# Audio tower kernel: attention and output weights loaded to the place of their low parts, the second chunk's norm split, one reciprocal moved

## What is computed

```python
h = xf @ W_proj + b_proj                     # token layer
y = layernorm(h) * ln_g + ln_b
w = softmax((y @ W_wgen + b_wgen).reshape(B, T, 8, 5))
conv = einsum('kbthr,bthk->bthr', taps(y), w)
h = h + relu(conv @ W_ff + b_ff)

x = layernorm(h)                             # attention, 8 heads of 64
q, k, v = split(x @ w_qkv.T + b_qkv)
attn = softmax(causal(einsum('bhfc,bhtc->bhft', k, q)), axis=-2)
h = h + (einsum('bhft,bhfc->bhtc', attn, v) @ w_o.T + b_o)

h = h + block_diagonal_ffn(layernorm(h))     # 16 blocks, GELU
```

## Time and profile before

| | |
|---|---|
| median of 3 runs | 1031.34 us (1030.89 to 1031.8) |
| the profiled execution's own time | 1035.96 us |
| its span | 1034.2 us |
| TensorE busy | 967.4 us, 94% of the span |
| VectorE, ScalarE, GpSimd busy | 509.2, 424.4, 394.3 us |
| mean granted TensorE clock | 0.977 of full speed |

### The profile page before, as it was taken

The page is one execution under the profiler, slowest core; times in us unless marked ns, Lnnn a source line. Parts: engine busy times, 40 slices in busy tenths (PEclk is TensorE's granted clock), DMA queues, the critical chain, the costliest instruction groups (busy, mean ns, idle before and its releaser), DMA issues.

```text
span 1034.2 us, 15644 instructions
## 1 busy us (share of the span) xinstructions
PE 967.4 (94%) x6108; PEld 714.5 (69%) x6108; DVE 509.2 (49%) x848; ACT 424.4 (41%) x753; POOL 394.3 (38%) x317
## 2 busy tenths in 40 slices
PE   7999999987899999999879999999999999889996
PEld 5777777776777788778657877877887777323331
DVE  6153535659447502254756256256064567755551
ACT  6144444555433533434243243243132332356553
POOL 1225252227601122723361451451023377748532
PEclk9999999999899999999989999999999999899998
DMA  8542725395343154327100201200214975533421
GB/s 290 209 165 4 205 7 181 4 285 203 117 145 107 62 126 164 109 95 265 41 11 22 92 11 35 79 11 22 92 52 149 289 260 209 184 111 133 149 77 61
DMA packets 75062, 124.96 MB, mean 121 GB/s; under 512 B 29159, under 2 KB 38375, under 8 KB 70894
## 3 DMA queue, kind: packets, MB, share of 16 engines
q1 hardware_dynamic: 68830, 107.03, 33.7%
q0 software_dynamic: 5120, 16.78, 4.6%
q10 hardware_dynamic: 1040, 0.16, 0.1%
HBM read 81.46 MB, written 42.50 MB: 120 GB/s over the span
## 4 chain that ended last, share of the span: by engine, by line
PE 53%; issue 10%; POOL 7%; DVE 5%; DMA 3%; ACT 2%; another core or an unknown queue 1%; POOLq 0%; SPq 0%; DVEq 0%; ACTq 0%
PE bank L299 14%; PE bank L301 13%; PE bank L300 13%; PE bank L1795 3%; PE bank L1804 3%; POOL vacc L335 2%; PE bank L1551 1%; POOL out L758 1%; POOL acc L363 1%; DVE sq L377 1%; DMA stage<-w_qkv_t 1%; POOL acc L308 1%; DVE acc L1219 1%; PE bank L1523 1%; DMA db_late<-h_s 1%
## 5 line engine op out<-in xcount | busy, mean ns | idle before, releaser
L335 POOL TENSOR_TENSOR vacc<-vacc,sq 128x512 f32<-128x512 f32 x72 | 97.2, 1350 | 45.8 <-ACT sq L381 36.4
L299 PE MATMUL bank<-xa_h,wp_h 128*128 128x512 f32 x256 | 103.4, 404 | 7.2 <-DVE xa_l L1094 7.2
L299 PE MATMUL bank<-cv_h,wf_h 128*128 128x512 f32 x256 | 106.3, 415 | 1.2 <-POOL wf_l L293 1.2
L301 PE MATMUL bank<-cv_h,wf_l 128*128 128x512 f32 x256 | 101.4, 396 | 0.0
L300 PE MATMUL bank<-cv_l,wf_h 128*128 128x512 f32 x256 | 101.4, 396 | 0.0
L300 PE MATMUL bank<-xa_l,wp_h 128*128 128x512 f32 x256 | 101.1, 395 | 0.0
L301 PE MATMUL bank<-xa_h,wp_l 128*128 128x512 f32 x256 | 101.1, 395 | 0.0
L700 POOL TENSOR_TENSOR fo<-fo,res 128x512 f32<-128x512 f32 x32 | 43.5, 1373 | 123.4 <-ACT fo L837 89.8
L1077 ACT ACTIVATE gt<-bank 128x512 f32<-128x512 f32 x128 | 66.2, 600 | 39.0 <-PE bank L1795 36.8
L1795 PE MATMUL bank<-dd,up_f 64*128 64x512 f32 x256 | 67.9, 651 | 5.6 <-ACT gt L1077 5.4
L381 ACT ACTIVATE sq<-sq 128x512 f32<-128x512 f32 x56 | 35.1, 632 | 79.3 <-DVE sq L377 79.3
(11 more groups left out here) (179 smaller groups left out, 2167.5 us busy)
## 6 DMA issues: line engine op xcount, KB each, us to landing
xs<-x_t SPq DMA_DIRECT2D x32, 256.0 KB, 6.2
h_s<-ho SPq DMA_DIRECT2D x8, 1024.0 KB, 5.9
res<-h_s SPq DMA_DIRECT2D x32, 256.0 KB, 3.6
h_s<-fo SPq DMA_DIRECT2D x32, 256.0 KB, 2.4
dc<-h_s SPq DMA_DIRECT2D x4, 2048.0 KB, 9.3
h<-h_s SPq DMA_DIRECT2D x8, 1024.0 KB, 10.5
h_s<-h SPq DMA_DIRECT2D x8, 1024.0 KB, 4.8
stage<-w_qkv_t SPq DMA_DIRECT2D x24, 256.0 KB, 3.6
```

The source lines that it names most:

```text
L299: pe.matmul(o, wh, xh, start=start, stop=False)
L301: return pe.matmul(o, wl, xh, start=False, stop=stop)
L335: g.tensor_tensor(vacc[:, :], t[:, 0, :] if k == 1 else vacc[:, :], t[:, k % 2, :], ALU.add).then_inc(ln_pool, 1)
```

## The change

Units from 32 on no longer go through `stage`. Each is loaded to the place where its low part will be written (`wv_r`, `wq_r`, `wk_r`, `wo_r` are float32 views of the low parts' places), so nine can be under way (RAW = 9). The places hold w_ff or the convolution's result until the last group of stage B has read them; TensorE counts that in a new semaphore `ff_used`, block by block, and the loads wait for it. Wv and wq have their high and low places exchanged. ScalarE writes the high parts of the first four wv units inside the last group, and those of all wq and wk units ahead of taking v out. `c_values(0)` waits for the first 28 results of stage B instead of all 32; the rest of that wait moves to `c_qk(0, 0)`. The load of chunk 1 comes after all 16 wq and wk units, and no longer after eight. The mean of chunk 1 is taken inside `c_qk(0, 0)`, and four of its eight blocks are centred and squared before q and k of pair 0 are taken out. In every chunk but the last the reciprocal of the next chunk's norm comes after k of pair 2 is taken out.

```diff
-        wv_h = place("wv_h", [P, KB, PART], F32R, R2)
-        wv_l = place("wv_l", [P, KB, PART], F32R, R2 + 16 * KIB)
-        wq_h = place("wq_h", [P, KB, PART], F32R, R2 + 32 * KIB)
-        wq_l = place("wq_l", [P, KB, PART], F32R, R2 + 48 * KIB)
+        wk_r = place("wk_r", [P, KB, PART], F32, R1 + 48 * KIB)
+        wv_l = place("wv_l", [P, KB, PART], F32R, R2)
+        wv_r = place("wv_r", [P, KB, PART], F32, R2)
+        wv_h = place("wv_h", [P, KB, PART], F32R, R2 + 16 * KIB)
...
+        def raw_load(e, u):
+
+            src, _, _, _, raw, dead = units[u]
+            if dead is None:
+                e.wait_ge(v_mm, 4 * CH)
+            elif dead == KB:
+                e.wait_ge(ff_mm, 8 * CH)
+            else:
+                e.wait_ge(ff_used, dead)
+            if u - RAW >= U_V:
+                who = 0 if units[u - RAW][3] == "v" else 1
+                e.wait_ge((w_lo_v, w_lo_g)[who], lo_before[who][u - RAW + 1])
+            e.dma_start(raw, src).then_inc(w_ld[(u - U_V) % RAW], 16)
...
-                if c == CH - 1:
-                    for u in range(U_V, U_V + 4):
-                        unit_load(sp, u)
                 for m in range(KB):
+                    if c == CH - 1:
+                        for u in {4: range(U_V, U_QK), 6: range(U_QK, U_QK + 2), 7: range(U_QK + 2, U_QK + 4)}.get(m, ()):
+                            raw_load(sp, u)
                     ff_store(c, m)
...
-            for u in range(U_V + 4, U_QK + 8):
-                unit_load(sp, u)
+            for u in range(U_QK + 4, U_O):
+                raw_load(sp, u)
             c_load(1)
-            for u in range(U_QK + 8, U_O):
-                unit_load(sp, u)
...
+                if not ahead:
+                    for k in range(4):
+                        act.wait_ge(ff_used, 4 + k // 2 + 1)
+                        unit_hi(act, U_V + k)
...
             c_values(0, range(TILES))
-            for u in range(U_V + 16, U_O):
-                unit_hi(act, u)
+            c_squares(1, range(4))
             c_qk(0, 0)
...
+            c_center(1, range(4))
             c_qk(0, 0)
...
                 if ahead:
-                    c_center(c + 1)
+                    c_center(c + 1, range(KB) if later else range(4, KB))
                 c_qk(c, 1)
                 c_softmax_in(c, 1)
                 c_softmax_out(c, 1)
+                if not ahead:
+                    o_low(0, range(PAIRS))
+                c_qk(c, 2)
                 if ahead:
                     since(v, ln_std, c + 1 + CH, 1, 1)
                     v.reciprocal(rstd[:, :], rstd[:, :]).then_inc(ln_rstd, 1)
-                else:
-                    o_low(0, range(PAIRS))
-                c_qk(c, 2)
...
-            c_qk(0, 0)
+            c_qk(0, 0, lambda: ln_mean_pe(pe, 1 + CH))
```

More of the change, by code:

```diff
@@ L140, in audio_tower @@
         wo_l = place("wo_l", [P, PAIRS, D], F32R, R2 + 16 * KIB)
+        wo_r = place("wo_r", [P, PAIRS, D], F32, R2 + 16 * KIB)
         vs_h = place("vs_h", [P, PAIRS, N], F32R, R1 + 16 * KIB)
@@ L161, in audio_tower @@
         masks_ok = sem("masks_ok")
-        stage_ld = [sem(f"stage_ld{i}") for i in range(4)]
+        w_ld = [sem(f"w_ld{i}") for i in range(RAW)]
+        ff_used = sem("ff_used")
         w_hi = sem("w_hi")
@@ L245, in weight_units @@
                     cols = slice(half * N, half * N + N)
-                    units.append((w_o_t[k * P:(k + 1) * P, cols], wo_h[:, k, cols], wo_l[:, k, cols], "g"))
+                    units.append((w_o_t[k * P:(k + 1) * P, cols], wo_h[:, k, cols], wo_l[:, k, cols], "g",
+                                  wo_r[:, k, cols], None))
             return units
@@ L273, in unit_load @@
             src = units[u][0]
-            e.dma_start(stage[:, u % 4, :], src).then_inc(stage_ld[u % 4], 16)
+            e.dma_start(stage[:, u % 4, :], src).then_inc(w_ld[u % 4], 16)
         def slot_count(u):
@@ L280, in unit_views @@
         def unit_views(u):
-            return stage[:, u % 4, :], units[u][1], units[u][2]
+            raw = units[u][4] if u >= U_V else stage[:, u % 4, :]
+            return raw, units[u][1], units[u][2]
         def unit_hi(act, u):
-            act.wait_ge(stage_ld[u % 4], slot_count(u))
+            unit_landed(act, u)
             st, h, _ = unit_views(u)
@@ L896, in _, with c_squares @@
                 unit_hi(act, u)
-            def c_squares(n):
-                for k in range(KB):
+            def c_squares(n, ks=range(KB)):
+                for k in ks:
                     ln_square_act(act, n + CH, k, dc[:, k, :])
@@ L989, in c_vals @@
                                    bias=vec[:, B_V + m:B_V + m + 1]).then_inc(vo_ev, 1)
-            for u in range(U_V, U_V + 16):
+            for u in range(U_V + 4, U_O):
                 unit_hi(act, u)
@@ L1014, in c_step @@
                 c_softmax_exp(c, 0)
+                if ahead and not later:
+                    c_squares(c + 1, range(4, KB))
                 if later:
@@ L1021, in c_step @@
                 c_pt(c, 0)
-                if ahead and not later:
-                    c_squares(c + 1)
                 c_softmax_exp(c, 1)
@@ L1245, in _, with c_center @@
                 b_step(c)
-            def c_center(n):
-                for k in range(KB):
+            def c_center(n, ks=range(KB)):
+                for k in ks:
                     ln_center_dve(v, n + CH, k, dc[:, k, :], dc[:, k, :])
@@ L1567, in ff_group @@
                         mm.then_inc(ff_mm, 1)
+                if g == 2 and c == CH - 1 and k < KB - 1:
+                    mm.then_inc(ff_used, 1)
             def b_step(c, ahead):
@@ L1620, in c_values @@
             def c_values(c, ts, beside=None):
-                if isinstance(c, int) and c == 0:
-                    pe.wait_ge(ff_ev, 8 * CH)
+                if c == 0:
+                    pe.wait_ge(ff_ev, 8 * (CH - 1) + TILES)
                 elif 2 in ts:
@@ L1645, in c_qk @@
                 first = isinstance(c, int) and c == 0
+                if m == 0 and first:
+                    pe.wait_ge(ff_ev, 8 * CH)
                 if m == 1 or (m == 0 and first):
@@ L1663, in c_qk @@
                         mm.then_inc(xc_used, 1)
-                    if beside and k == 3:
+                    if beside and k == (5 if m == 0 else 3):
                         beside()
@@ L1716, in c_step @@
                     c_values(c, (2, 3))
-                if ahead:
+                if ahead and later:
                     ln_mean_pe(pe, c + 1 + CH)
@@ L1841 @@
 LAST_PREP = {0: (4, 5), 1: (6, 7)}
+RAW = 9
 PREP_AFTER, STAT_FROM, GATHER_AFTER = 3, 5, 4
```

23 lines of the change are left out of this document (17 added, 6 removed).

## The result

The changed kernel takes **1044.95 us**, median of four runs (1040.25 to 1046.14); the kernel before took 1031.12 (1030.55 to 1031.8, four runs). The medians lie 13.8 us apart. The ratio of the runs is 1.0125, with a 95% interval of 1.0105 to 1.0145, which is 12.9 us: slower, and clear of the noise. The forecast was 1041.0 us (1029 to 1047), slower by 9.7, with a chance of 0.73 for slower. The profiled execution took 1046.14 us and is the slowest of the four.

A forecast was written before the change was run, and what follows sets the result against it. TensorE, busy 94% of the span, was taken to bound the kernel. Gains of 10.4 us against 20.1 lost to the moved reciprocal gave +9.7 on a median of 1031.34: 1041.0 us, range 1029 to 1047.

The forecast's parts named there:

- Start of stage C: From stage B's last matmul to the first of `c_values(0)`: the wait goes, 2.3 us gained.
- First q and k group: `c_qk(0, 0)`: no longer starves on low parts, 15.8 us falls to the 10.9 needed, 4.8 us gained.
- Mean of chunk 1: Inside `c_qk(0, 0)`: chunk 1's load issued about 475, sum done at 494, a wait of 0.3 us, up to 3.
- Rival 4: Chunk 1's load lands late and PE waits about 4.5 us at the mean, plus 1.7 slow clock: 1047 us; chance 0.05.
- first case: All terms as summed, the moved reciprocal costing waits and clock: slower, 1041 us (1037 to 1046); chance 0.62.
- Squares ahead of q: Ahead of the first scores: four squares delay q, PE waits 3.0 us instead of 0.94, 2.1 us lost.
- Clock: Behind the new 3.0 us wait ahead of the first scores: a half-speed stretch costs 1.7 us.
- Variance: Variance of chunk 1: the wait of 5.2 us and 2.2 us of lower clock go, 7.4 us gained.
- Moved reciprocal: Ahead of pair 3's scores, chunks 0 to 2: 4.5 us wait plus 2.2 clock each, 20.1 lost; E ends k's take-out.
- Rival 3: Faster: VectorE and GpSimd hardly disturb each other, a chunk loses under 4.0 us; 1024 us (1022 to 1030); chance 0.18.
- Rival 2: The moved reciprocal costs the wait but not the clock: +1.4 us, 1033, up to 1036; chance 0.15.
- Output weights: Their loads wait for the last `c_values`, about 742, and are first read near 758: no effect.

The follow-up runs named there:

- units_ahead: Changed kernel with the reciprocal back in its old place and more q and k units issued ahead of two stage B stores; 1024.9 us, ratio 0.9913.
- ahead_q_first: As units_ahead, with q of pair 0 also taken out ahead of the four squares of chunk 1; 1023.2 us, ratio 0.9901.
- recip_back: Changed kernel with the reciprocal put back ahead of k of pair 2, all else as changed; 1023.0 us, ratio 0.9896 to the kernel before.
- no_lock: Changed kernel with low parts of xc for chunks 1 to 3 subtracting a PSUM bank, so VectorE reads one SBUF input; 1032.1 us, ratio 1.0002.
- fill_pe: Changed kernel with 24 unused matmuls in the wait ahead of pair 3's scores of chunks 0 to 2; 1037.8 us, ratio 1.0046.
- recip_alone: Kernel before with only the reciprocal moved behind k of pair 2; 1053.1 us, ratio 1.0193.
- norm_alone: Kernel before with only the norm of chunk 1 split (earlier mean, four blocks centred and squared early), old weight loads and reciprocal; 1027.4 us, ratio 0.9954.
- q_first: Changed kernel, reciprocal back, chunk 1's load behind the first eight q and k units, first q taken out ahead of four squares; 1021.7 us, ratio 0.9906.

## Why the prediction was right, point by point

The direction, the main term and its three places were right, and the range held the time. The sum was 4.1 us short of the medians and 3.2 short of what the two traces add up to (12.9). The 3.2 come from two terms: the start of stage C gained 8.9 instead of 10.4, and the moved reciprocal cost 21.8 instead of 20.1.

- **Start of stage C**: forecast 2.3 gained. Before, PE went from the last matmul of stage B to `c_values(0)` in 2.61 us, now in 0.23: 2.4. Right.
- **First q and k group**: forecast 4.8. The 36 matmuls ahead of the mean ran without a gap: 487.30 + 36 x 0.228 = 495.5, and the mean started at 498.73 after its wait of 3.11. Right.
- **Mean of chunk 1**: forecast a wait of 0.3, measured 3.1. This is the step that failed. It had SP issue the load of chunk 1 about 475, by ScalarE's pace of 0.63 us for a high part; ScalarE was not the pace: it waited for landings, and SP stood at a store from 464.5 to 468.85. The prediction cost what the wv loads delay "at nothing" and looked only at the residual loads; fourteen units stood behind the stores that wait for those. The queue's part is about 1.2 us by units_ahead and ahead_q_first; for the rest the traces show full DMA engines and low parts at the slow pace, and no run separates the two. Rival 4 of the prediction had named this wait (4.5 us) and gave it 0.05: half of it came true beside the first case, so the prediction was right with this step wrong, because the wait is small beside the main term.
- **Squares ahead of q**: forecast 3.0 of wait instead of 0.94. It was 1.52 (2.45 in recip_back): PE, at the lower clock behind the mean, reached the end of the group later, so part of that wait was already spent. In recip_back the clock behind the mean was full.
- **Clock**: forecast 1.7, behind the wait ahead of the first scores. It was lost behind the mean instead. The mean and the twelve matmuls behind it took 5.3 us (498.73 to 504.07, the end of the group by its last matmul at 503.84) where 0.45 + 12 x 0.228 = 3.2 were needed: 2.1. That this came near the forecast is partly luck: recip_back, with waits of 3.48 and 2.45 in the same places, had full clock behind both. The prediction sorted such waits by length, nothing after 2.22 and a slow stretch after 2.5 or more; over all traces that does not hold under 4 us (last section). The sum of these: 2.4 + 4.8 - 3.1 - 0.6 - 2.1 + 7.5 = 8.9, which is what the two traces show; forecast 10.4.
- **Variance**: 7.4 forecast, 7.5 measured.
- **Moved reciprocal**: forecast 4.5 of wait and 2.2 of clock in each of three chunks, 20.1. Measured 4.9 and 2.4, 21.8. The chain was right step by step (GpSimd from E + 3.3, four low parts beside the last scalings at 1.7, four alone in 2.4, scores at E + 19.1, the late end of the range given). With the strict lock of 1.85 a pair the prediction had 5.6 of waiting a chunk; the pairs took 1.7 and the waiting was 4.9. Rival 3, a loss under 4.0 a chunk, fell with the traces: 7.3. no_lock shows what its premise would have given: two engines that leave each other alone lose 2.0 a chunk in waiting, and the time is that of the kernel before (1.0002), not 1024. Waits of 3.2 that still cost the clock are the likely reason, but only one execution was traced, and it had one such stretch (1.5 us) in three chunks. Rival 2, a wait without the clock, is about what fill_pe measures: 1038, not the rival's 1033, since the start of stage C gained less and the waits were longer.
- **Output weights**: nothing, as forecast. The last scores of chunk 3 stand 254.4 us ahead of the end in the profiled execution of before and 249.9 in that of the changed kernel; but recip_alone and norm_alone, which load them in the old way, have 248.1 and 249.7, and the other ten traces, with the new loads, 247.8 to 250.1. So the 4.5 us are that one execution's own, about the 4.6 by which it lies above its median. They are why the spans of the two traces differ by 10.2 us only: 12.9, and 1.8 from ahead of stage C, less 4.5.

The measured difference (13.8) and the one summed from the traces (12.9) differ by less than the spread of the four runs. One slip of the prediction changes nothing: its first case, by its own terms, runs from 1038 to 1045 and not from 1037 to 1046.

## What to carry to other kernels

An instruction that runs in an idle gap of its engine costs nothing there. Moved out of the gap into the chain, it costs what is left of its length after the slack (here 2.0 us of 3.3), plus what its successors lose when they now run beside an engine that slows them (2.9), plus the clock behind a wait that has grown (2.4). So ask of each move which gap it leaves and what it makes simultaneous; here 3.3 us of work cost 7.3. The version to keep is the change without the move of the reciprocal, about 1% faster than before (0.9896 [0.9842, 0.9951]); the variants around it can't be told from it. And before a load is put behind others, look at the DMA share of the stretch: here, at 1.0, three orders gave the same time, and the order only chose who waits.

## What the runs showed of the hardware

- Whether the clock falls behind a wait of PE of 2.2 to 3.9 us cannot be told from its length. The fourteen traces have nineteen such waits in stage C: a slow stretch came behind ten of them and full clock behind nine. Behind 2.22 us it was 0.51 in norm_alone, 0.65 in ahead_q_first and 1.00 in the kernel before; behind 3.48 in recip_back 1.00, behind 3.86 in q_first 0.65; behind three waits of 3.20 in no_lock 0.53, 1.00 and 1.00.
- Ten waits of 5.1 to 6.1 us all had a slow stretch behind them (0.50 to 0.54 at its start). Its length differed: 0.72 over 6.6 us in one chunk of the changed kernel and 0.54 and 0.55 in the others, for the same wait, which is 1.65 us lost against 2.75 and 2.66.
- VectorE with two SBUF inputs and GpSimd, each 128x512 in float32, took 1.7 us a pair, where 0.6 and 1.25 one after the other would be 1.85. With one input from PSUM, VectorE's were 0.64 apart and GpSimd's stayed at 1.34 on average.
- A reciprocal of 128x512 in float32 takes 3.34 us on VectorE, five times a subtraction of that size (0.68).
